# The experts' first block: the two copies of router logits move from VectorE to ScalarE

## The reference

```
x = x + layernorm(mamba(layernorm(x)))
h = layernorm(x)
# experts
logits = einsum("bsd,ed->bse", h, gate_w)              # 16 experts
scores = softmax(logits, axis=-1).transpose(0, 2, 1)
topk_w, topk_idx = top_k(scores, cap)                  # cap = 256 * 2 / 16 = 32 tokens for each expert
out = scatter_add(expert(gather(h, topk_idx)) * topk_w)
# shared expert, for every token
shared = (gelu(h @ Ws_g.T) * (h @ Ws_u.T)) @ Ws_d.T
x = x + layernorm(out + shared)
```

## Time and profile before

| | |
|---|---|
| time, median of three runs | 1394.62 us (1392.88, 1394.62, 1401.41) |
| the profiled execution's own time | 1400.59 us |
| its span, first to last instruction | 1398.9 us |
| TensorE, VectorE, ScalarE, GpSimd busy | 78%, 79%, 64%, 67% |
| mean granted TensorE clock | 0.892 |
| VectorE's copies of logits (L1004) | 2, of 0.69 us, at 978.4 and 1008.7 us |

### The profile page before, as it was taken

One profiled execution on the slowest core, in us unless ns is written; L12 is line 12 of the kernel. 1 busy time (PEld: TensorE's weight loads), 2 busy tenths in 40 slices (PEclk: granted clock), 3 DMA queues, 4 the chain that ended last, 5 costly groups with the idle time before them and its releaser, 6 DMA issues. The chain is left out here.

```text
span 1398.9 us, 15385 instructions
## 1 busy us (share of the span) xinstructions
PE 1094.9 (78%) x4128; PEld 510.1 (36%) x4128; DVE 1103.3 (79%) x1440; ACT 889.4 (64%) x1614; POOL 938.9 (67%) x503
## 2 busy tenths in 40 slices
PE   4667878787777878777777876445998989999796
PEld 2322222222222222222222322133755336666695
DVE  7499999999999999999999999896382962222288
ACT  3567577667667677667667665356332866666796
POOL 0199999999999999999999999722010740000176
PEclk9878899989999899989998898867798999999898
DMA  5745835834834835834834836110000001111013
GB/s 159 152 101 112 183 71 111 182 81 101 182 77 105 182 75 107 182 85 97 182 81 101 183 81 162 41 31 1 1 0 23 1 1 34 44 35 34 12 31 91
DMA packets 48490, 122.87 MB, mean 88 GB/s; under 512 B 5824, under 2 KB 20928, under 8 KB 42304
## 3 DMA queue, kind: packets, MB, share of 16 engines
q1 hardware_dynamic: 46864, 121.01, 39.1%
q10 hardware_dynamic: 1584, 1.36, 0.3%
HBM read 83.55 MB, written 5.24 MB: 63 GB/s over the span
## 5 line engine op out<-in xcount | busy, mean ns | idle before, releaser
L555 POOL TENSOR_TENSOR states<-b_dup,dup 128x1024 f32<-128x1024 f32 x256 | 596.5, 2359 | 63.3 <-DMA dup<-dd 61.7
L648 DVE TENSOR_TENSOR_SCAN da<-da,states 128x1024 f32<-128x1024 f32 x160 | 359.5, 2283 | 38.7 <-ACT da L397 32.6
L397 ACT ACTIVATE da<-dup,decay 128x510 f32<-128x510 f32 x512 | 327.2, 672 | 11.1 <-DVE states L648 11.1
L295 PE MATMUL yp<-states,fold 128*64 128x512 f32 x1024 | 275.4, 664 | 15.6 <-DVE states L574 9.8
L534 POOL TENSOR_TENSOR states<-states,X 128x1024 f32<-128x1024 f32 x96 | 226.1, 2356 | 20.5 <-DVE states L648 20.4
L648 DVE TENSOR_TENSOR_SCAN states<-da,states 128x1024 f32<-128x1024 f32 x96 | 218.7, 2278 | 7.0 <-ACT da L397 7.0
L574 DVE TENSOR_TENSOR states<-da,X 128x1024 f32<-128x1024 f32 x160 | 192.5, 1203 | 0.0
L1664 POOL TENSOR_SCALAR put<-row_t,slot_i,slot_w 128x256 f32<-128x256 f32 x32 | 39.1, 1222 | 193.3 <-POOLq L1368 173.5
L393 ACT ACTIVATE da<-zeros 128x4 f32<-128x4 f32 x177 | 30.5, 173 | 197.2 <-DVE states L574 196.3
L295 PEld LDWEIGHTS yp<-states,fold 128*64 128x64 f32 x1024 | 69.4, 152 | 212.5 <-issue 196.2
L1469 DVE TENSOR_TENSOR hx<-glx,upx 128x512 f32<-128x512 f32 x64 | 41.3, 684 | 126.6 <-ACT glx L1434 118.2
(11 more groups left out here) (185 smaller groups left out, 1779.9 us busy)
## 6 DMA issues: line engine op xcount, KB each, us to landing
b_dup<-bc_rows SPq DMA_DIRECT2D x32, 1024.0 KB, 9.6
dup<-dd SPq DMA_DIRECT2D x128, 256.0 KB, 11.7
X<-bc_rows SPq DMA_DIRECT2D x64, 512.0 KB, 11.5
out<-X SPq DMA_DIRECT2D x3, 1024.0 KB, 5.1
wg<-in_wgT SPq DMA_DIRECT2D x16, 128.0 KB, 2.1
wu<-in_wuT SPq DMA_DIRECT2D x16, 128.0 KB, 2.2
wd<-in_wdT SPq DMA_DIRECT2D x16, 128.0 KB, 2.2
bc_rows<-bcf SPq DMA_DIRECT2D x16, 64.0 KB, 1.6
```

Source lines behind the costliest of these rows:

```text
L295: last = nc.tensor.matmul(yp[64 * i:64 * i + 64, :], fold[:], states[:, (2 * step + i) % RING, s, :], start=False, stop=(q == 3 and s == S ...
L397: ins = nc.scalar.activation(factors[:, s, :].rearrange("p (b t) -> p b t", b=2)[:, :, 1:S], src[:, :, 1:S], ACT.Exp, scale=decay[:, col:c ...
L555: nc.gpsimd.tensor_tensor(states[:, i % RING], b_dup[:, par, s0:s0 + SPI, :], dup[:, par, 1, h, g, :].unsqueeze(1).broadcast_to([P, SPI, N ...
L648: nc.vector.tensor_tensor_scan(to.rearrange("p s t -> p (s t)"), factors.rearrange("p s t -> p (s t)"), ring.rearrange("p s t -> p (s t)") ...
```

## The change

`take_logits` is removed from VectorE's program and written into ScalarE's, as an activation `Copy` with the same operands and the same semaphores. ScalarE takes the first bank at n = 8, right behind turned(8) and ahead of scaled(15), and the second one behind its loop over the pairs, after evacuate(4) and ahead of gelu(5, 0). VectorE took the first one at n = 9, behind products(2). TensorE's, GpSimd's and SyncE's programs stay as they are.

```diff
@@ scalar
+                def take_logits(half):
+                    act.wait_ge(lp_ready, LP * (half + 1))
+                    nc.scalar.activation(L[:, CH * LP * half:CH * LP * (half + 1), :], lp[:].rearrange("p (c e) -> p c e", e=E),
+                                         ACT.Copy).then_inc(lp_free, 1)
...
                     if n == STARTS[3] - 2:
                         nc.scalar.preload_act_table_set(LOG_EXP)
                         inverse_x(3)
+                    if n == LP:
+                        take_logits(0)
                     for s, q in SCALED_AT:
                         if n == s:
                             scaled(q)
...
                     if n and n % 3 == 0:
                         evacuate(n // 3 - 1)
+                take_logits(1)
                 for m in range(EARLY, PAIRS):
                     gelu(m, 0)
@@ vector
-                def take_logits(half):
-                    dve.wait_ge(lp_ready, LP * (half + 1))
-                    nc.vector.tensor_copy(L[:, CH * LP * half:CH * LP * (half + 1), :], lp[:].rearrange("p (c e) -> p c e", e=E)
-                                          ).then_inc(lp_free, 1)
...
                         products(n // 3 - 1)
-                    if n == LP + 1:
-                        take_logits(0)
                     if n == STARTS[1] + 1:
...
-                take_logits(1)
                 dve.wait_ge(lp_free, 2)
```

## The result

The changed kernel took 1391.68 us (median of 22 runs, 1389.34 to 1393.80), the kernel before 1394.55 in the same rounds (22 runs, 1392.64 to 1401.41). The ratio is 0.9977 with a 95% interval of 0.9970 to 0.9985: 2.1 to 4.2 us faster. The forecast was 1392.8, or 1.8 us faster. The direction holds, and the time lies in the stated range of 1390.0 to 1400.0. That range is over three times as wide as the gain. The forecast gave its own step 0.9 to 2.5 us; the gain of 2.9 lies just above that, with an interval that reaches back into it.

What follows compares the result with a forecast made beforehand. TensorE's instruction stream was taken as the bound from 979.21 to 1008.62 us, behind its 9.2 us wait. Logits moved 1.70 plus copy 0.60 minus new copy 0.48 gave 1.82; median 1394.62 less that is 1392.8 us, range 1390.0 to 1400.0.

Steps and rivals of the forecast that it cites:

- its own step: Experts' first block: moving the first copy gains 0.9 to 2.5 us, taken as 1.8; chance 78%.
- The wait and what takes its place: TensorE's 9.2 us wait moves to products(2), 7 to 8 us long; down projection starts 1.82 us sooner.
- The second copy: On ScalarE before gelu(5, 0): costs and brings nothing; VectorE's reduction may start 0.1 us earlier.
- The clock behind the hole: Full clock returns 3 to 4.5 us behind pair 3's first gate matmul; gain 0.9 to 2.5 us, taken as 1.8.
- if the return stays where it was: Clock still returns at 993.84, so the lead of 1.82 us at half clock is worth 0.91.
- The prediction's own sign: Wrong if pair 5's second gelu is not 1 to 2.5 us earlier beside pair 8's transposes.
- A shift at 1009 should reach the end: Stretches behind VectorE's exponential wait follow without slack, so time gained at 1009 us should reach the kernel's end.
- The rival of the missed clock: Clock misses pair 3's gate and up matmuls, returning only with pair 4: 7.1 us slower, 1401.7; chance 4%.
- Against the profiled execution: Whole kernel: 1400.59 us of the profiled run less 1.82 gives 1398.8.
- The rule in the Trainium skill: First copy on ScalarE: were it three times 0.69, or 2.07 us, the gain would be an estimated 0.2 us.

Runs made afterwards that it cites:

- the first copy alone: Changed kernel with the second copy of logits back on VectorE, only the first on ScalarE: 1392.93 us, ratio 0.9987.
- the profile shown: Profile of the unchanged kernel on which the prediction was made; that profiled execution took 1400.59 us.
- the second profile of before: Unchanged kernel profiled and timed once more, nothing edited: 1395.26 us (12 runs).
- the delayed kernel: Changed kernel plus two more 128x512 ScalarE activations at the block's end, rewriting gl with itself: 1394.64 us against 1391.40 for the changed kernel.
- the three comparisons: The changed kernel, unedited, measured three times against the kernel before: 1391.68, 1391.54 and 1391.40 us; ratios 0.9977, 0.9971 and 0.9968.
- down first: Kernel before with the down projection of pair 2 put ahead of pair 8's logits on TensorE: 1403.49 us, ratio 1.0039.
- the kernel before, filled: Kernel before plus nine TensorE matmuls of 512 columns, results overwritten, in the hole ahead of pair 8's logits: 1391.94 us, ratio 0.9975.

## Why the prediction was right, and where not

- **The wait and what takes its place: right.** The logits run in the hole, TensorE waits for products(2), 7.5 us long, and resumes 1.90 us sooner; 1.82 were forecast. The 0.48 us that the copy costs in ScalarE's queue are measured three ways: 970.30 to 970.78 in the timeline, and 9.77 against 9.28 in two kernels without it.
- **The second copy: right in the trace.** Nothing is late behind it, VectorE's reduction starts 0.09 us earlier (0.1 was forecast), and the sum gains nothing. In the timed runs it is not settled.
- **The clock behind the hole: the step that was mis-sized.** The prediction put the return 3.1 to 4.5 us behind the first gate matmul of pair 3, moving with it, and took 1.8. In the profile of a common run it is back before those matmuls. It came 14.75 us behind pair 8's transposes before (982.84 less 968.09), and 14.74 with the first copy alone: the same instant, in two profiles of the same group. (In the changed kernel's it is 14.37, 14.37 and 14.36; they are of another group.) That was the low end of the forecast's span, "if the return stays where it was": a lead of 1.89 us at half clock, worth 0.94 at full. The two profiles that share the instant say 0.98 at the sum (40.29 less 39.31). So the direct gain is 1.0 us in such a run, not 1.8. Only against the late return of the profile shown is it 5.95.
- **Where the placing of the return went wrong: a row was left out.** The prediction measured "the three other places where it came back in this block" and read that it comes back "only with gate and up matmuls". There is a fourth, in the same trace:

```profile
959.70:963.11 3.41, 3.41 (x17) 3.41 (x17) 3.41 (x8) 2.46 (x9) 1.98 (x2) 0.50 0.00 0
963.11:965.88 2.77, 2.77 (x29) 2.77 (x27) 1.53 (x5) 2.34 (x7) 0.42 (x1) 1.00 0.02 6
```

```profile
959.99 3.52 PE L1133 MATMUL yp<-wsdT,hs 128*128 128x128 f32 x16
...
965.88 0.68 PE L1124 MATMUL gp<-xhT,wsgT 128*128 128x512 f32 x1
```

There the clock returned at 963.11, with down matmuls running and 2.77 us ahead of the next gate matmul. In the changed kernel it came back 2.01 us ahead of that matmul (984.19 and 986.20).
- **The prediction's own sign says so.** It would be wrong, it said, if pair 5's second gelu was not 1 to 2.5 us earlier beside pair 8's transposes. Against the profile shown it is 5.95 us earlier (42.09, now 36.14). Against the second profile of before (37.30) it is 1.16.
- **"A shift at 1009 should reach the end": it does, and grows.** Against the second profile of before, the gain up to the gather stage is 1.1 to 1.3 us (104.23 against 102.94 to 103.17), of which up to 0.2 goes with the group and not with the change. There the dip of the clock is 3.41 us long in place of 6.83, worth 1.4 to 1.6, and the last stage is 0.5 to 0.7 us shorter. From the fourteen profiles, a fall 2.9 us or less behind the stage's first matmul goes with the long dip, 3.3 or more with the short one, without exception; the delayed kernel turns one into the other. It is not the earlier, the better: with the clock up through the block the changed kernel comes 2.4 us sooner still (100.79) and meets the long dip again. The sum is 3.3 us (423.31 from pair 8's transposes to the end, against 419.95 to 420.08), which fits the 2.9 to 4.2 of the three comparisons. So the median agrees with the forecast's size in part by luck: the direct step gave about half of the 1.8, and steps that the forecast did not have, the shorter dip and the shorter last stage, gave the rest and more. The last stage has a difference in the clock too: the dip about its start is 10.24 us long in the seven profiles with the long dip, and 6.83 in the seven others. What makes one follow the other was not tested.
- **The rival of the missed clock** did not occur: in no profile did the return come later than 24.60 us behind pair 8's transposes, where the rival had it at 36.9. What did occur is the return at 24.60 of the profile shown, which the forecast took for the usual one. Up to the gather stage it costs 6.4 us against the return of the second profile. The kernel before has 16 of 132 runs that lie as high; of the changed kernel's 46 none is over 1395.9. Why the changed order never meets it, and down first seems to (its nine runs all lie at 1398.0 or over), is argued from what TensorE runs and not shown.
- **Against the profiled execution the sum was far off:** 1400.59 less 1.8 is 1398.8, and the changed profile had 1391.57. Forecasting against the median is why it came out near: the late return in that profile is worth more than the change.
- On the clock, the Trainium skill, page "TensorE: Matmul & The Clock Gate", part on the clock gate, says that the watch on activity runs freely and isn't started by the kernel. The traces agree that its changes keep their instants when work moves by 2 us. They also stand in a few fixed places to the kernel's own work: in the fourteen profiles the first fall came 1.4, 2.6 or 3.3 us behind the block's start, and nowhere else.
- The rule in the Trainium skill, page "ScalarE: Activation LUTs", section "Rules for kernel authors", that gives cheap elementwise work to VectorE, did not bite: 0.60 to 0.62 us on ScalarE, 0.69 on VectorE. But VectorE's early copy did as well as any on ScalarE.

## What to carry to other kernels

When an engine stands idle, look at which of its next instructions could already run, and what holds them; here one 0.69 us copy stood behind a 7.7 us wait that it had nothing to do with, and its place mattered, not its engine. A lead won while the clock is at half is worth half, unless the clock's return moves too. Before sizing an effect of a few microseconds, take a second profile of the unchanged kernel, and follow the gain through every stage behind: here a shift of 1 us came with another length of a dip 67 us behind VectorE's sum, and the two came out as 3. And put side by side only profiles in which the clock did the same ahead of the edit.

## What the runs showed of the hardware that was not expected

- The clock's changes can stay at the same instants while the work under them moves by 1.9 us (14.75 and 14.74 us behind pair 8's transposes, with and without the first copy in VectorE's queue). Dips come in two lengths, 3.41 and 6.83 us at the gather stage.
- The clock fell while TensorE was busy. In the profile shown before it fell at 1065.52, behind 24.72 of 24.72 us busy (from 1040.80), with matmuls of 8 columns running for the last 2.4:

```profile
1040.80:1065.52 24.72, 24.72 (x131) 16.03 (x129) 9.49 (x16) 8.33 (x14) 1.11 (x2) 1.00 0.00 1
```

- It did so again in the kernel before, filled, where it fell at 981.47: 2.8 us behind the nine filling matmuls, 1.4 us behind TensorE's resuming, with logits of 16 columns and down matmuls running.
- It came back with no gate or up matmul since its fall: at 963.11 in the profile shown before, with down matmuls running, and at 984.19 in the changed kernel, with logits running behind down matmuls and transposes.
- Exchanging 16 down matmuls with eight of logits, with TensorE resuming 2.4 us sooner, made the kernel 5 us slower by the ratio (1.0039) and 8 us at the median (1403.49 against 1395.34), with the clock's return 24.60 us behind pair 8's transposes.
